# Gated stage: routing masks ahead of the first cumulative sum, the keys' exponential and route rows ahead of ScalarE's exponentials, the second mask later

## The reference

```python
q1, k1, v = heads(x @ Wq) * scale, heads(x @ Wk), heads(x @ Wv)          # 8 heads of 64
q2 = heads(x @ Wqa @ Wqb) * scale
k2 = softmax(heads(x @ Wka @ Wkb), axis=-1)
gk1, gk2 = log_sigmoid(x @ Wg1a @ Wg1b + bg1) / 16, log_sigmoid(x @ Wg2a @ Wg2b + bg2) / 16
e = softmax(x @ We);  mask = one_hot(top_1(e));  rw = e * mask           # 4 routes
# gated linear attention, per chunk of 64 tokens:
def chunk_gla(q, k, v, gk):
    g = cumsum(gk);  qg, kg = q * exp(g), k * exp(-g)
    o_intra = tril(qg @ kg.T) @ v
    # state:  S = S * exp(g_last) + (k * exp(g_last - g)).T @ v;   o_inter = qg @ S
    return o_intra + o_inter
o = chunk_gla(q1, k1, v, gk1) + sum_over_routes(chunk_gla(q2 * rw_r, k2 * rw_r, v, gk2 * mask_r))
o = o * rsqrt(mean(o * o) + eps) * norm_w * silu(x @ Wga @ Wgb)
x = x + o @ Wo
```

## Time and profile before

| | us |
|---|---|
| runs shown, median (lowest to highest, 3 runs) | 1873.02 (1871.5 to 1876.74) |
| the profiled execution's own time | 1868.34 |
| its span, first to last instruction | 1867.0 |
| TensorE busy | 1602.5 |
| VectorE busy | 1274.1 |
| ScalarE busy | 1112.6 |
| GpSimd busy | 694.0 |

### The profile page before, as it was taken

The page is one execution under the profiler, slowest core; times in us unless marked ns, Lnnn a source line. Parts: engine busy times, 40 slices in busy tenths (PEclk is TensorE's granted clock), DMA queues, the critical chain, the costliest instruction groups (busy, mean ns, idle before and its releaser), DMA issues. The chain is left out here.

```text
span 1867.0 us, 45497 instructions
## 1 busy us (share of the span) xinstructions
PE 1602.5 (86%) x19664; PEld 1016.7 (54%) x19664; DVE 1274.1 (68%) x2035; ACT 1112.6 (60%) x1654; POOL 694.0 (37%) x500
## 2 busy tenths in 40 slices
PE   4678888999989989989987778888887888899999
PEld 2355665677677767766774223433343343466665
DVE  4665745666666667666775868778877887756664
ACT  3265666766776676667752467667667767533221
POOL 4213202444344244434540355464556555411100
PEclk8798998999999999999996889999999999999999
DMA  7855100000000000000015055137236222000000
GB/s 184 213 141 128 17 15 1 2 2 2 1 2 2 2 2 2 2 1 2 22 72 118 24 187 128 48 109 164 70 91 161 73 65 70 23 7 12 6 12 12
DMA packets 43357, 102.30 MB, mean 55 GB/s; under 512 B 3944, under 2 KB 12288, under 8 KB 41428
## 3 DMA queue, kind: packets, MB, share of 16 engines
q1 hardware_dynamic: 40244, 93.88, 19.3%
q10 hardware_dynamic: 2912, 5.51, 1.6%
HBM read 67.12 MB, written 31.46 MB: 53 GB/s over the span
## 5 line engine op out<-in xcount | busy, mean ns | idle before, releaser
L1450 DVE TENSOR_REDUCE arena<-ring 128x2 f32<-128x1024 f32 (+2 forms) x320 | 341.9, 1109 | 89.3 <-PE ring L1307 63.1
L1550 ACT ACTIVATE arena<-ring 128x1024 f32<-128x1024 f32 (+1 forms) x320 | 291.5, 938 | 133.7 <-PE ring L1336 89.8
L2505 POOL TENSOR_TENSOR arena<-arena 128x1280 f32<-128x1280 f32 x28 | 65.3, 2333 | 344.3 <-PE accs L2271 284.4
L1357 PE MATMUL accs<-arena 128*9 128x512 f32 (+3 forms) x1536 | 174.0, 526 | 2.7 <-ACT arena L1550 2.6
L1300 PE MATMUL ring<-arena 48*128 48x512 bf16 (+3 forms) x768 | 130.2, 350 | 42.9 <-DVE arena L1450 20.5
L1329 PE MATMUL ring<-arena 51*128 51x512 bf16 (+3 forms) x768 | 125.3, 344 | 43.7 <-DVE arena L1450 24.2
L2497 POOL TENSOR_TENSOR arena<-arena 128x512 f32<-128x512 f32 x112 | 141.2, 1293 | 3.0 <-DVE arena L2312 3.0
L292 POOL TENSOR_SCALAR xn<-x,moments,rstd 128x128 f32<-128x128 f32 x80 | 64.5, 823 | 196.9 <-DVE rstd L263 181.4
L2772 ACT ACTIVATE arena<-ring 128x512 f32<-128x512 f32 x80 | 47.8, 597 | 147.3 <-PE ring L2627 140.5
L2490 POOL TENSOR_TENSOR arena<-arena 128x1024 f32<-128x1024 f32 x32 | 82.2, 2570 | 112.7 <-DVE arena L2365 112.7
L2732 DVE TENSOR_TENSOR arena<-arena,ring 128x512 f32<-128x512 f32 x80 | 55.0, 687 | 87.9 <-PE ring L2629 74.5
(11 more groups left out here) (346 smaller groups left out, 4249.0 us busy)
## 6 DMA issues: line engine op xcount, KB each, us to landing
arena<-whole_k SPq DMA_DIRECT2D x32, 512.0 KB, 4.7
arena<-whole_q SPq DMA_DIRECT2D x32, 512.0 KB, 6.4
arena<-c_scratch_q SPq DMA_DIRECT2D x14, 384.0 KB, 8.3
arena<-c_scratch_k SPq DMA_DIRECT2D x14, 384.0 KB, 11.0
a_scratch_k<-arena SPq DMA_DIRECT2D x8, 512.0 KB, 4.1
c_scratch_k<-arena SPq DMA_DIRECT2D x8, 512.0 KB, 4.4
arena<-a_scratch_q SPq DMA_DIRECT2D x9, 384.0 KB, 6.4
arena<-a_scratch_k SPq DMA_DIRECT2D x9, 384.0 KB, 8.7
```

The lines of the kernel that those rows point to most:

```text
L1357: mm = nc.tensor.matmul(acc[ci % 2][32 * h:32 * h + HD + 1, a - c * BANK:BANK], c_values[b % 2][:, j, r * HEADS // 2 + 2 * g + i, :], weig ...
L1450: nc.vector.tensor_reduce(dst, src, AX.X, ALU.max, negate=True).then_inc(c_max_taken.up(item), 1)
L1550: nc.scalar.activation(view(c_probs[wi % 4]), view(ps), ACT.Exp).then_inc(c_weights_made.up(item), 1)
```

## The change

The list gets a new place for three things. `mx` moves from behind `soft` to just ahead of the first `sum`, with `k2x` in front of it. The two strips of route rows become an item of their own, `half`, right behind `pair`. The second mask becomes an item `mask`, behind `mx`. `rows_w` of the next batch moves from behind the first `sum` to behind `pair`, and the causal stage's `low` and `write` from the place of `mx` to behind the second `sum`. Four of the norm's table loads are no longer issued. No matmul, vector or activation instruction is added or dropped beside these loads.

```diff
-            7: {"sum0": [("rest", 0, "k")], "kt": [("mid", 0, "k")], "mx": [("low", 0, "k"), ("write", 0, "k")]}}
+            7: {"sum0": [("rest", 0, "k")], "kt": [("mid", 0, "k")], "sum1": [("low", 0, "k"), ("write", 0, "k")]}}
...
-                act_norm(s, item[1], item[1] == 0)
+                act_norm(s, item[1], False)
...
-                act_norm(s, t)
+                act_norm(s, t, t == 0)
...
-                              7: {"sum0": [("rows_w", c)]}}[tile]
+                              7: {"pair": [("rows_w", c)]}}[tile]
...
-            order = [("z", 0), ("pair", -1), ("gk", 0), ("k2x", 0), ("mx", 0), ("sum", 0, 0), ("soft", 0), ("sum", 0, 1),
+            order = [("z", 0), ("pair", -1), ("gk", 0), ("half", 0), ("k2x", 0), ("mx", 0), ("sum", 0, 0), ("soft", 0), ("sum", 0, 1),
...
-                round_ = [("pair", i), ("sc", i, 0), ("sc", i, 1), ("sum", n, 0), ("k2x", n), ("kt", i), ("soft", n), ("mx", n),
-                          ("fin", i - 1), ("sum", n, 1), ("qk1", n), ("vk", n), ("z", n + 1), ("routed", n), ("kv", i, 0),
-                          ("kv", i, 1), ("av", i), ("in", i, 0), ("in", i, 1), ("mid", n), ("gk", n + 1)]
+                round_ = [("pair", i), ("half", n), ("sc", i, 0), ("sc", i, 1), ("k2x", n), ("mx", n), ("mask", i),
+                          ("sum", n, 0), ("kt", i), ("soft", n), ("fin", i - 1), ("sum", n, 1), ("qk1", n), ("vk", n),
+                          ("z", n + 1), ("routed", n), ("kv", i, 0), ("kv", i, 1), ("av", i), ("in", i, 0), ("in", i, 1),
+                          ("mid", n), ("gk", n + 1)]
...
-                    elif kind == "sc":
-                        i = item[2]
-                        dv.wait_ge(gla_scored, (t, i))
+                    elif kind == "sc" and item[2] == 0:
+                        dv.wait_ge(gla_scored, (t, 0))
...
+                    elif kind == "mask":
+                        dv.wait_ge(gla_scored, (t, 1))
+                        dv.wait_ge(mix_made, (t, "tril"))
...
-                    elif kind == "mx":
-
+                    elif kind == "half":
                         if t:
                             ac.wait_ge(sum_mm, (t - 1, 1))
                         ac.wait_ge(route_step, ((s, t // NT), "hot"))
...
+                    elif kind == "mx":
                         ac.wait_ge(mix_mm, t)
```

More of the change, by code:

```diff
@@ L2355, in dve_program @@
                                                        decay[t % 3][:, :, 1, :], ALU.mult, ALU.mult).then_inc(state_step.up((t, "factor")), 1)
-                    elif kind == "sc":
-                        i = item[2]
-                        dv.wait_ge(gla_scored, (t, i))
+                    elif kind == "sc" and item[2] == 0:
+                        dv.wait_ge(gla_scored, (t, 0))
                         if t:
                             dv.wait_ge(gla_weighed, t - 1)
[L2361 to L2364, removed]
                         nc.vector.tensor_tensor(
-                            masked[i][:, :].rearrange("p (h c) -> p h c", c=P), src[:, :].rearrange("p (h c) -> p h c", c=P),
-                            mask.unsqueeze(1).to_broadcast([P, GLA_HEADS, P]), ALU.mult).then_inc(gla_masked.up((t, i)), 1)
+                            masked[0][:, :].rearrange("p (h c) -> p h c", c=P), ps[:, :].rearrange("p (h c) -> p h c", c=P),
+                            w("tril").unsqueeze(1).to_broadcast([P, GLA_HEADS, P]), ALU.mult).then_inc(
+                            gla_masked.up((t, 0)), 1)
+                    elif kind == "mask":
+                        dv.wait_ge(gla_scored, (t, 1))
+                        dv.wait_ge(mix_made, (t, "tril"))
+                        if t:
+                            dv.wait_ge(gla_weighed, t - 1)
+                        nc.vector.tensor_tensor(
+                            masked[1][:, :].rearrange("p (h c) -> p h c", c=P), accs[:, :].rearrange("p (h c) -> p h c", c=P),
+                            mix_tril[t % 2][:, :].unsqueeze(1).to_broadcast([P, GLA_HEADS, P]), ALU.mult).then_inc(
+                            gla_masked.up((t, 1)), 1)
                     elif kind == "kv":
```

## The result

The changed kernel took 1818.53 us (median of 4 runs, 1815.79 to 1823.18), the kernel before 1872.26 us in the same job: a ratio of 0.9724, 95% interval 0.9703 to 0.9745. The direction was right, the size too small. Both medians here are of four runs. The kernel before took 1867.95 to 1869.46 us in the three jobs of the experiments (7 to 13 runs each) and the changed kernel 1818.7 in one of them, which makes the gain about 51 us, and the 1873.02 that the forecast was taken off some 4 us too high.

What follows compares the result with a forecast made beforehand. TensorE was taken to bound the gated stage, busy 649.81 of 722 us. 41.6 + 5.9 - 5.3 + 1.4 - 3.6 = 40.0 us off the 1873.02 us median gave 1833 us, range 1825 to 1850 for eight in ten.

Steps and rivals of the forecast that it cites:

- Waits gone less those given back: Gated stage: TensorE loses 41.6 us of waits in 37 places; later VectorE work gives back 5.3 us.
- the 1.6 us for the first score mask: Turning of the keys waits about 0.08 us for the first mask product in some 20 tiles: 1.6 us given back.
- VectorE's part: Give-back where the head mean's scaling stands until GpSimd's join ends, so decayed keys hold the outer products: 3.7 us.
- Overlap: Each of 37 removed TensorE stops also loses 0.16 us of overlap between matmul groups: 5.9 us gained.
- The clock: Two TensorE stops, near 627 and 952 us, had lower-clock stretches of about 1.4 us behind them; half taken: 1.4 us gained.
- Waits that I don't see: Tighter order at `hot_b`, the first sum's slot and `mx`: 3.6 us lost, about 0.1 a tile, between 0 and 12.
- The end of the stage, taken as 0: Last tile: `low` and `write` placed behind the previous head mean cost nothing, between -1 and +1 us.
- rival E: Slower: TensorE's granted clock in the stage falls from 0.98, each 0.01 costing about 7 us; 0.90 gives 1885. Chance 0.05.
- rival R: Posed with the experiments: gain beyond TensorE's idle time comes from the matmuls' new order, the clock has no part.
- Rival B: VectorE and GpSimd take over the pace; head mean's scaling 0.55 us later: 25 us saved (13 to 34), 1848. Chance 0.27.
- D: More than 46 us saved, 1820 to 1827: the give-back does not come, the clock stays up in both places. Chance 0.06.

Runs made afterwards that it cites:

- tables_only: The kernel before with only the four norm table loads left out: 1861.0 us, ratio 0.9956 to the kernel before.
- after_again: The changed kernel run once more, unedited: 1818.7 us, ratio 0.9730 to the kernel before.
- stops_long: The changed kernel with seven more copies of `hot_b` on ScalarE in the fourth tile of each batch: 1840.52 us, ratio 0.9852 to the kernel before.
- before_again: The kernel before run once more, unedited, for a second trace: ratio 1.0001 to the kernel before.
- gates_behind_mx: The changed kernel with the gates hung behind the routing masks in place of the second scores: 1819.45 us, ratio 0.9740 to the kernel before.

## Why the prediction was wrong in its size

It was right in its mechanism and wrong in three terms of its sum. The stage gave 51.3 us where the sum had 40.0:

- *Waits gone less those given back*: 41.6 - 5.3 = 36.3 forecast; the two lists give 72.4 - 36.2 = 36.2 us. Right. Within the give-back the 1.6 us for the first score mask did not come (L2221 starts 1.02 us behind L2208 in tile 19, before 1.00), VectorE's part was larger, 5.6 us for 3.7, the waits for `hot_b` were 0.6 longer, and the join's was 1.0 shorter.
- *Overlap*: 5.9 forecast, from 0.16 us for each of 37 stops. Left over are 51.3 less 36.2 and 7.5 for the clock, 7.6 us; 1.7 too small. Most of it can be read tile by tile: in tiles 1 to 30, with the slow stretches of 15 and 30 left out, the lengths fell by 7.2 us more than the idle time. Neither factor was right. The lists have 63 stops before and 33 after (without L1260's), 30 fewer, since new ones came at L2246; and each was worth more than 0.16. In tile 17 a stop of 1.00 us went and the tile is 1.34 shorter: 0.16 is the overlap, 0.08 the group behind the stop, which took 1.17 us and takes 1.09, and 0.07 the head mean, which took 1.10 and takes 1.02 though no stop stood in front of it.
- *The clock*: 1.4 forecast. The step that failed most is "I take half". The kernel before had four such stretches in the stage; the prediction had rows of only two and took half of them. Tile 15 lost 1.66 us (23.17 for 21.51), tile 30 1.63 (22.76 for 21.13 in tables_only), tile 31's `av` and `in` 2.95 (1.97 + 4.48 for 1.09 + 2.41), tile 0 about 1.3 (an estimate: 1.59 beyond its idle time, less 0.3 for a stop that went). That is some 7.5 us, and the changed kernel's trace had none of the first three and less in tile 0. 6.1 too small. The 1.4 us for one stretch was too small as well, for it counts the L2213 group alone. In after_again tile 31 keeps 1.1 us of it.
- *"Waits that I don't see"*: -3.6 forecast, without a row. The only one that came is 0.2 us in tile 0 (L2208). 3.6 too large.

1.7 + 6.1 + 3.6 - 0.1 = 11.3 us, the stage's miss. The last 2.4 us between 51.3 and 53.7 are within the interval. The end of the stage, taken as 0, is in these terms already: the join ended 1.0 us earlier and the clock stayed up behind the shorter stop, 3.7 us in tile 31 together (2.6 in after_again).

Two slips changed nothing. L2170 is the first product of the routing masks, not a transpose. And at 7 us for each 0.01, a clock of 0.90 in rival E would cost 56 us and give 1889, not 1885.

That the clock is the cause of slow groups behind stops is shown by repetition (the same group fast in one trace and slow in the next, with the granted clock beside it) and by stops_long. Of the 7.2 us, what is overlap and what is rival R's closer order is told apart in tile 17 only, where R has the 0.07. Rival B (VectorE and GpSimd take over the pace) came no further than the give-back of the sum: L2246 waits 8.3 us, but L2396 ends 10.84 us into tile 19 where it was 10.83, not 0.55 later, and the 25 us saved were far off. E did not come: the clock of 300 to 930 us is 1.00 at 96% busy (604.10 of 630). D, more than 46 us, is where the time fell, and it had 0.06. Of its two conditions one held: the give-back came, the clock stayed up. The second should have weighed more, since both slow stretches that the prediction had rows of stood behind stops that the change removes.

Part by part, leaving out the loads is worth 5.2 us in the kernel before; putting them back into the changed kernel cost 5.7 and 3.3 more for the clock. The exponential's new place is worth nothing, and that of `low` and `write` 1.3 to 2.4. The rest, some 40 us, is put down to the masks and route rows ahead of the first sum, with the ring order that follows from them, by subtraction and by the waits that went. No run moved the masks, the route rows, the second mask or `rows_w` alone.

## What to carry to other kernels

Price a stop of the pacing engine by more than its idle time: look at what runs right behind it, group against the same group elsewhere, and count every slow stretch before the sum is made. Take no allowance for waits that no row shows out of the middle of the sum; it belongs to the range. And where one engine paces a hand-written order, side work of another engine goes behind what the pacing engine waits for, not ahead of it: here that made the stage another 9.7 us shorter, and 15.3 with the gates moved too.

## What the runs showed of the hardware

Behind TensorE's stops the next groups ran at the lower clock in some executions and not in others, at identical stops. Of 1.96 to 1.97 us (tiles 7, 15 and 23 of the kernel before, in before, before_again and tables_only) three of nine had it; of 2.14 us (tile 30 of the same) two of three. Of 2.6 us (tile 31 of the changed kernel and of those made from it) six of nine had it: not the first trace of the changed kernel, stops_long and gates_behind_mx. All four of 3.37 us had it, and all four of 3.56 to 3.58. Two stops of 0.53 and 1.15 us close together had it in two tiles of four. A stretch cost 1.1 to 3 us.

ScalarE's table load cost 1.28 us and no drain: a tile was 1.31 us shorter without it and 1.43 longer with it. The Trainium skill, ScalarE: Activation LUTs, "What ACT_TABLE_LOAD costs", has 2.66 us for load and drain at every switch to a different set. The four loads of the norm were of a set already in place, so the runs that move them don't test the page's case. In the traces the loads behind the gates (L2425, in the changed kernel L2431), which do switch the set, start 0.02 us behind the instruction before them, take 1.28 us, and the next one starts 0.01 us behind them; there the measurement, 1.31 us in all, differs from the page and decides here.
